# Cross-attention phase of a decoder layer: memory and token transposes moved from TensorE to DRAM round trips and VectorE

## The reference, cut to what matters

```
x   = x + attn(layernorm(x), ...)                          # phase A
x   = x + xattn(layernorm(x), ctx_1024, mask, ...)         # phase B
x   = x + ffn(layernorm(x), ...)                           # phases C and D

def xattn(x, mem_seq, mem_mask, rms_scale, q_w, kv_w, out_w):
    xn, mn = rmsnorm(x, rms_scale), rmsnorm(mem_seq, rms_scale)
    q      = rope(xn @ q_w) * HEAD_DIM**-0.5               # 4 heads of 128
    k, v   = mn @ kv_w ;  k = rope(k)                      # one head
    probs  = softmax(where(mem_mask, q @ k.T, MASK_FILL))
    return (probs @ v) @ out_w
```

## Time and profile before

| | |
|---|---|
| median of 3 runs | 3075.41 us (3075.34 to 3076.96) |
| the profiled execution | 3076.55 us, its span 3074.8 us |
| TensorE busy | 3035.9 us, 99% |
| VectorE busy | 1889.9 us, 61% |
| ScalarE busy | 1272.4 us, 41% |
| GpSimd busy | 830.7 us, 27% |
| phase A, 27 to 826 us | TensorE 797.1 of 799.0 us, VectorE 617.0, DMA engines 53% busy |
| phase B, 826 to 1860 us | TensorE 1014.5 of 1034.0 us, VectorE 801.9, ScalarE 665.2, GpSimd 634.2 |

### The profile page before, as it was taken

How to read it: one execution, slowest core, us unless ns; L and a number is a source line. 1 busy time by engine, 2 the same in 40 slices (tenths; PEclk the granted TensorE clock), 3 DMA queues, 4 the chain that set the end, 5 groups by cost and what they waited for, 6 DMA issues and landing times.

```text
span 3074.8 us, 40217 instructions
## 1 busy us (share of the span) xinstructions
PE 3035.9 (99%) x15124; PEld 2559.6 (83%) x15124; DVE 1889.9 (61%) x4077; ACT 1272.4 (41%) x2419; POOL 830.7 (27%) x699
## 2 busy tenths in 40 slices
PE   8999999999999999999999989999999999999999
PEld 7888888888878888888888878888888888888887
DVE  6777878777687778877877775343323343332455
ACT  4434343434366667666666652221211221112243
POOL 0101010101256666666666640000000000000144
PEclk9999999999999999999999999999999999999999
DMA  4545555555512121212111232111111112111486
GB/s 151 141 148 141 151 138 151 137 156 132 173 70 71 56 96 58 71 56 98 63 64 69 71 110 69 55 55 53 58 42 42 41 57 55 54 28 45 141 291 225
DMA packets 229729, 298.32 MB, mean 97 GB/s; under 512 B 12960, under 2 KB 109216, under 8 KB 229536
## 3 DMA queue, kind: packets, MB, share of 16 engines
q1 hardware_dynamic: 229536, 295.76, 31.7%
HBM read 183.52 MB, written 97.52 MB: 91 GB/s over the span
## 4 chain that ended last, share of the span: by engine, by line
PE 96%; DVE 2%; issue 1%; ACT 1%; DMA 0%; POOL 0%; SPq 0%; DVEq 0%; ACTq 0%
PE c_p L130 11%; PE c_p L132 11%; PE c_p L131 11%; PE a_p L130 6%; PE a_p L131 6%; PE a_p L132 6%; PE b_n L130 5%; PE b_n L132 5%; PE b_n L131 5%; PE b_t L1679 3%; PE d_p L132 2%; PE d_p L131 2%; PE d_p L130 2%; PE a_p L990 2%; PE a_r L132 2%; PE a_r L130 2%
## 5 line engine op out<-in xcount | busy, mean ns | idle before, releaser
L1299 POOL TENSOR_SCALAR b_soft<-b_soft,b_one_in_sum 128x512 f32<-128x512 f32 x256 | 401.8, 1571 | 298.9 <-DVE b_one_in_sum L1482 298.9
L1933 ACT ACTIVATE c_gate<-c_p,c_bias 128x512 f32<-128x512 f32 x180 | 124.2, 690 | 682.5 <-PE c_p L132 682.5
L1963 DVE TENSOR_TENSOR c_gate<-c_gate,c_gate 128x512 f32<-128x512 f32 x64 | 44.2, 690 | 502.7 <-ACT c_gate L1933 502.7
L1501 DVE TENSOR_TENSOR b_p_lo<-b_t,b_p_hi 128x512 fp32r<-128x512 f32 x256 | 175.1, 684 | 159.1 <-ACT b_p_hi L1356 156.5
L1347 ACT ACTIVATE b_soft<-b_soft,b_minus_top 128x512 f32<-128x512 f32 x256 | 185.2, 723 | 181.0 <-DVE b_minus_top L1493 176.4
L351 POOL TENSOR_TENSOR kept_scale<-c_ln_ve,minus_half 128x4 f32<-128x4 f32 x16 | 16.2, 1010 | 880.0 <-DVE c_ln_ve L343 880.0
L1356 ACT ACTIVATE b_p_hi<-b_t 128x512 fp32r<-128x512 f32 x256 | 151.8, 593 | 107.6 <-PE b_t L1679 107.6
L617 ACT ACTIVATE a_elu<-a_p 128x512 f32<-128x512 f32 x128 | 75.6, 590 | 282.0 <-PE a_p L132 282.0
L351 POOL TENSOR_TENSOR a_ln_sc<-a_ln_ve,minus_half 128x4 f32<-128x4 f32 x16 | 16.3, 1019 | 626.8 <-DVE a_ln_ve L343 626.8
L1493 DVE CUSTOM_DVE_ANT_0 b_soft<-b_l,b_mask_row 128x512 f32<-128x512 f32 x256 | 175.2, 684 | 0.0
L1679 PE MATMUL b_t<-ident,b_soft 128*128 128x128 f32 x1024 | 154.3, 273 | 12.2 <-DVE b_p_lo L1501 11.1
(11 more groups left out here) (297 smaller groups left out, 9520.6 us busy)
## 6 DMA issues: line engine op xcount, KB each, us to landing
a_res<-in_x SPq DMA_DIRECT2D x16, 1024.0 KB, 6.5
x<-a_res SPq DMA_DIRECT2D x16, 1024.0 KB, 5.2
b_mem<-in_ctx SPq DMA_DIRECT2D x16, 1024.0 KB, 5.4
b_x<-x SPq DMA_DIRECT2D x16, 1024.0 KB, 5.5
b_res<-x SPq DMA_DIRECT2D x16, 1024.0 KB, 5.5
x<-b_res SPq DMA_DIRECT2D x16, 1024.0 KB, 4.5
c_x<-x SPq DMA_DIRECT2D x16, 1024.0 KB, 5.6
d_x<-x SPq DMA_DIRECT2D x16, 1024.0 KB, 5.6
```

What stands on the lines that cost most here:

```text
L1299: pool.tensor_scalar(soft[:, at, :], soft[:, at, :], one_in_sum[:, at:at + 1], None, ALU.mult).then_inc(p_norm.sem, p_norm.unit)
L1501: dve.tensor_tensor(part.low, pT_bank[:, :].rearrange("p (i s) -> p i s", i=T), part.high_f32(), ALU.subtract).then_inc(p_lo.sem, p_lo.unit)
L1933: act.activation(gate[j % 2][i][:, :], gating.banks[(3 * j + i) % 6][:, :], ACT.Tanh if g == "c" else ACT.Sigmoid, bias=added[:, i, j:j + ...
```

## The change

In phase A, ScalarE squares the memory of each batch as it comes from DRAM (only the row sums are kept), while a second, shuffled copy is loaded; VectorE turns it with four 32x32-transpose instructions, and it is stored turned, not scaled, to DRAM (`x2`). The shuffled tokens of phase A go back into `x` itself and the shuffled attention output into `att`. One GpSimd pair of instructions makes the memory's scales of all batches.

In phase B the turned memory is loaded into `memT_f`, split into `memT` in slots 6 to 9 (high, ScalarE), 9 and 10 (low, chunks 0 and 1, GpSimd) and 14 and 15 (low, chunks 2 and 3, VectorE), and `keys_values(0)` waits for all four. Its scale is applied to the keys and values: `values_high` becomes four ScalarE instructions of 128 columns with a scale operand in place of one of 256. The rotation of the keys reads `k_scaled`, in SBUF, in place of the PSUM bank.

The tokens of batches 1 to 15 are normalised by ScalarE (slot 15, two tiles, and slot 0, two tiles), stored to DRAM, read back shuffled into `x`, turned by VectorE into `nT_f` in slots 5 to 8 ahead of `p_low`, and split: high by ScalarE in slots 5 to 8, low by GpSimd in slots 6, 7 and 8 (two in slot 8). Batch 0 is turned by TensorE as before. The larger jobs are placed anew.

```
-            Q, MEM = KT + 1, KT + 1 + H
+            Q = KT + 1
             jobs = [(k_rope, 2, 0), (k_rope, 6, 0)]
             for t in range(T):
                 jobs += [(xT_lo, t, 0), (x2_sb, t, 2)]
-            jobs += [(k_lo, 0, 0)] + [(q_cos, h, 0) for h in range(H)] + [(memT_lo, c, -1) for c in range(C)]
+            jobs += [(k_lo, 0, 0)] + [(q_cos, h, 0) for h in range(H)]
...
+            def shuffle_x(sp, b):
+                sp.wait_ge(N.normed.sem, N.normed.upto(b))
+                sp.dma_start(self.token_rows(self.out, b), x[:, :, :]).then_inc(x_moved.sem, x_moved.unit)
+                sp.wait_ge(x_moved.sem, x_moved.upto(b - 1, 0))
+                self.load_shuffled(sp, x, self.out, b, x_moved)
...
+                    def tokens_low(c):                      # GpSimd
+                        pool.wait_ge(xT_hi.sem, xT_hi.upto(new.b, c))
+                        pool.tensor_tensor(nT.low[:, c, :], nT_f[:, c, :], nT[:, c, :].high_f32(), ALU.subtract).then_inc(xT_lo.sem, xT_lo.unit)
...
                     for j in range(J):                      # GpSimd
                         if old and j < J - 1:
                             normalise(old.b, j + 1)
...
+                            if new.b >= 1 and 6 <= j <= 8:
+                                tokens_low(j - 6)
+                                if j == 8:
+                                    tokens_low(C - 1)
...
-                            if j == 9:
+                            if j == 10:
                                 query_sin(new.b, 0)
...
+                            if j == 9 or j == 10:
+                                memory_low(pool, after, j - 9)
...
+                            act.activation(v[new.par].high[:, t, :], bank[:, i, HD:2 * HD], ACT.Copy, scale=mem_scale[:, new.b, t:t + 1]).then_inc(v_hi.sem, v_hi.unit)
+                            act.activation(k_scaled[:, t, :], bank[:, i, 0:HD], ACT.Copy, scale=mem_scale[:, new.b, t:t + 1]).then_inc(v_hi.sem, v_hi.unit)
...
                         dve.wait_ge(v_hi.sem, v_hi.upto(new.b, 4 * g + 3))      # VectorE, keys(g)
...
                         if new and j == J - 1:              # VectorE
                             one_over(new.b, 0)
+                        if new and new.b >= 1 and 5 <= j <= 8:
+                            tokens_turned(j - 5)
                         if old and j >= 1:
                             p_low(old.b, j - 1)
...
+                            if j >= 14:
+                                memory_low(after, j - 12)
...
+                        if g == 0:                          # TensorE, keys_values(g)
+                            pe.wait_ge(mem_lo.sem, mem_lo.upto(new.b))
...
                         if new and j == 2:                  # TensorE
-                            keys_values(1)
+                            keys_values(1, (0,))
...
+                        if new and j == 3:
+                            keys_values(1, (1,))
+                        if fin and outs <= j < outs + T:    # outs is 4
+                            out(j - outs)
...
-                        if old and j == 7:
-                            encode(old, 0)
                         if new and j == 7:
                             turn_keys()
-                        if new and j == 8:
+                        if old and j == 8:
+                            encode(old, 0)
+                        if new and j == 9:
                             queries(0)
-                        if new and j == 9:
+                        if new and j == 10:
                             queries(1)
-                        if old and j == 10:
+                        if old and j == 11:
                             encode(old, 1)
-                        if new and j == 11:
+                        if new and j == 12:
                             queries(2)
...
+                        if after and j == 13:
+                            queries(3, (0, 1))
+                        if after and j == 14:
+                            queries(3, (2, 3))
...
-                        if following(new, B) and j in (13, 14):
-                            turn_memory(pe, s, new.b + 1, 2 * (j - 13))
-                            turn_memory(pe, s, new.b + 1, 2 * (j - 13) + 1)
```

More of the change, by code:

```diff
@@ L648, in step @@
                         weight_high(WQ, 2)
+                        for t in range(T):
+                            memory_square(act, new.b, t)
                     for c in range(C):
@@ L799, in step @@
                         weight_low(WP, 2)
+                        memory_turned(dve, new.b)
                     if old:
@@ L1307, in query_low @@
                         pool.tensor_tensor(q.low[:, h, :], rope[:, h % 2, :], q[:, h, :].high_f32(), ALU.subtract).then_inc(q_lo.sem, q_lo.unit)
+                    after = new.b + 1 if following(new, B) else None
+                    older_goes_on = old and following(old, B)
                     for j in range(J):
@@ L1438, in step @@
                                 query_high(new.b, 3)
-                        if new and 4 <= j <= 7:
-                            tokens_high(j - 4)
-                        if after and j >= 14:
-                            memory_high(act, s, after, 2 * (j - 14))
-                            memory_high(act, s, after, 2 * (j - 14) + 1)
+                            first = 4 if new.b == 0 else 5
+                            if first <= j < first + C:
+                                tokens_high(j - first)
                         if old and j < J - 2:
@@ L1554, in step @@
                     after = new.b + 1 if following(new, B) else None
+                    older_goes_on = old and following(old, B)
+                    sums = 5 if old else 4
                     for j in range(J):
@@ L1726, in turn_keys, with queries @@
                         mm.then_inc(kT_ps.sem, kT_ps.unit)
-                    def queries(h):
-                        bank = bank_of(Q + h)
-                        for c in range(C):
+                    def queries(h, chunks=range(C)):
+                        bank = bank_of(Q + h) if chunks[0] == 0 else turns.bank(s, Q + h)
+                        for c in chunks:
                             if h == 0:
@@ L1733, in queries @@
                             mm = product(pe, bank[:, :], qw[:, c, h * HD:(h + 1) * HD], nT[:, c, :], c == 0, c == C - 1)
-                        mm.then_inc(q_ps.sem, q_ps.unit)
+                        if chunks[-1] == C - 1:
+                            mm.then_inc(q_ps.sem, q_ps.unit)
+                    after = new.b + 1 if following(new, B) else None
+                    outs = 4 if old else 3
                     for j in range(J):
```

405 lines of the change are left out of this document (201 added, 204 removed).

## The result

The changed kernel takes 3124.32 us (median of 4 runs, 3122.74 to 3126.27) against 3075.72 beside it: ratio 1.0158, 95% interval 1.0146 to 1.017, slower by 48.6 us. The forecast was 3091, in a range of 3050 to 3110: the sign is right, the time lies outside the range. The profiled execution took 3125.27 us, its span 3123.5.

The account below looks back on a forecast made before the run. The prediction took TensorE's own queue, busy 99%, as the bound. From the profiled 3076.55 us, - 55.7 + 41 + 19 + 11 = 3091.9, so 3091 for the median, slower by 0.5%, in a range of 3050 to 3110.

Parts of the forecast that it names:

- What is removed: TensorE's memory and token transposes, 27.8 and 26.4 us, plus a 1.5 us wait for memory's split: gain at most 55.7 us.
- (a): Slot 7: `turn_keys` waits for GpSimd's low part of token chunk 2, 2.7 us in 15 steps, 41 us.
- (b): Slot 2: `turn_p(2)` waits for a late `p_low(1)`, 1.35 us in 14 steps, 19 us.
- (c): Slot 0: `keys_values(0)` waits for VectorE's low part of memory chunk 3, 0.7 us, 15 times, 11 us.
- What is hidden: Phase A's added squares, transposes and DMA, and phase B's token round trip, cost nothing; up to 1 us a phase A step.
- Rival 1: Slot 7's bank wait does not bite: 3050, or 3029 with the other waits at lower bounds; chance 0.15.
- Rival 2: Slot 7's wait bites, but those of slots 2 and 0 lie at their lower bounds: 3070; chance 0.19.
- Rival 3: Tokens' DRAM round trip comes late at `tokens_turned(0)`, slot 5; 15 us per us late, 3122 at 2 us; chance 0.08.

Follow-up runs that it names:

- experiment 11: Changed kernel with the repairs of experiment 1, experiment 4 and experiment 7 together, memory's low parts left in slots 14 and 15: 3041.16 us.
- experiment 1: Changed kernel, but bank bookkeeping skips the tokens' jobs 2, 4, 6, 8 from step 1 on, so `turn_keys` no longer waits for `xT_lo`: 3070.83 us.
- experiment 7: On top of experiment 1, memory's keys and values parted: keys scaled and rotated in slot 1, values' high and low parts in slot 2, slot 4 likewise: 3047.94 us.
- experiment 9: On top of experiment 1, experiment 4 and experiment 7, VectorE writes memory's low part 2 in slot 9 and part 3 in slot 14: 3032.56 us.
- experiment 5: On top of experiment 1, VectorE writes memory's low part of chunk 3 in slot 14 behind chunk 2, not in slot 15: 3067.97 us.
- experiment 4: Changed kernel, but the loads of memory 0 stand behind the load of batch 1's tokens in SyncE's queue: 3117.31 us.
- experiment 3: Changed kernel, but in GpSimd's slot 8 the low part of token chunk 2 stands ahead of `normalise(9)`: 3082.28 us.
- experiment 10: Changed kernel, but GpSimd does the memory's low part 0 in slot 8 ahead of token chunks 2 and 3, lengthening the `turn_keys` stall: 3151.42 us.
- experiment 6: On top of experiment 1, `values_high(0)` and `keys(0)` moved from slot 1 to slot 2: 3056.63 us.

## Why the prediction was wrong

By its own steps:

- **What is removed**, 0.87 and 0.44 us each time: right in the steady steps. Free of (a) and (b) a step is 57.87 (experiment 11) with (c) still in it, 0.64: 57.23 would be left, and 60.69 - 1.74 - 1.76 = 57.19. In step 1 the tokens' part bought nothing: it has no `out` products, and its slots 1 to 6, where the loop through `p_low` and `exp` sets the pace, took 18.24 before and 18.23 after. The prediction took every transpose at its spacing in a steady step.
- **(a)**, 2.7 us: right, 2.75 in steps 2 to 15, by the very chain that was written down. In step 1, whose slots are shorter and where TensorE was at the lower clock (granted 0.50 from 905 to 915 us), the slot took 8.71 (4.37 before, 3.27 in experiment 1).
- **(b)**, 1.35: right, 3.95 against 2.56, 1.39. Its cause was given as the end of `encode(fin, 3)` and more ScalarE work, and both are there: `p_low(1)` starts 3.22 after t(1), 0.95 later than before (2.27), by the added instructions, and ends at +3.89 (forecast 3.9). Of the two the waiting is the one that can be taken away: with the same work and no wait experiment 7 has `p_low(1)` at +1.27. Four ScalarE instructions started 0.25 apart, under the 0.3 that I took.
- **(c)**, 0.7: the size is right, 4.64 against 4.00, in part by luck. Changed kernel, between steps 5 and 6 (t(14) is 1194.33):

```profile
1197.43 0.94 DVE L1549 TENSOR_TENSOR b_memT_lo<-b_memT_f,b_memT_hi 128x512 fp32r<-128x512 f32 x1
...
1198.52 0.35 PE L130 MATMUL b_n<-b_kvw_hi,b_memT_hi 128*128 128x256 f32 x1 [0.39 <-DVE b_memT_lo L1549]
```

  The low part ends at +4.04: the chain's 3.8 and 0.25 more, 0.94 against 0.69 in slot 14. It begins 0.28 behind the start of GpSimd's `normalise`; beside no GpSimd instruction it took 0.68 (experiment 9). The prediction weighed in up to 0.9 for that, from a row beside a GpSimd instruction with two inputs in SBUF, which `normalise` is not, and took a value between. Beside one with two, in experiment 5, the same subtraction took 1.78 and ended 0.54 behind GpSimd's end; here it lost some 0.25 and did not wait for the end of `normalise`, which came 0.35 later than its own.
- **What is hidden**: the step that failed. "Phase A gets per step four ScalarE squares, four VectorE transposes and 3 MB of DMA [...] I take nothing" looked at a middle step, and there it holds: TensorE has no new wait. But SyncE's queue before the first step was not read, though 2 MB are put ahead of the tokens of batch 1 there. Forecast were 4.3 us less up to step 1, measured 8.5 more. Of these 12.8 us, 9.3 are there when TensorE waits for `a_att` (79.65 against 70.38), and experiment 4's order takes all of them away (69.66). What the order costs differs from run to run: 7.0 by the medians, 8.0 by the mean starts of step 1, and this trace, 4.1 later than the mean of its kind, is the dearest of eight. The other 3.5 arise behind that wait: just ahead of step 1 `keys_values` stands 2.5 us for the memory's low part, where (c) had 0.7, and the rest is not taken apart. "Phase A shows no new wait of TensorE" was wrong at the start, by the 5.67 us for `a_Wq_lo`.
- **Not in the sum at all**: the granted clock. The prediction priced a wait at its own length. Here a TensorE idle of 2.54 us brought half clock behind it in 5 of 13 steady steps, about 8 us, and over the doses the falls grew with the idle stretch: none of 13 behind 0.35 us (experiment 3), all 13 behind 3.76 (experiment 10). No single one of these explains the miss of 33 us: 3124.3 less the start's 12.8 is 3111.5, less the clock's 8 it is 3116.3, both still over 3110. The rest of the miss is step 1 (7.7: slot 7 takes 4.3 more than before, slot 8, again at the lower clock, 1.7, the others 1.6 and nothing is saved), 1.8 in steps 2 to 14 (a step at full clock grew by 1.45, not 1.32), step 15 (1.2, which no run takes apart), and 2.0 behind, in which a slot of the last step, 5.54 us, fell to the lower clock too (3.94 in experiment 6), behind an idle of 2.58 us; what brings it there in some traces and not in others stays open.

Rival 1 put the bank wait at 41 us. Experiment 1 shows it worth about 51, by the clock and step 1. Rival 2 is out by (b) and (c) as measured, 1.39 and 0.64, far over their lower bounds. Rival 3 did not come: VectorE never stood for a DMA at `tokens_turned`.

## What to carry to other kernels

When a buffer's writer goes away, its place in the bookkeeping must go too: a wait for nothing, asked one slot early, cost about 51 us, nearly all of the 54 that taking out 496 transposes was to give. Price a stall of TensorE by its length and by the clock behind it (here 2.54 us idle, and about 1.6 more in 5 of 13 steps), and look for what can be asked one slot later, or be parted so that only the piece that must wait stands behind the wait. Read the start of a program as a stage of its own: a load put ahead of another in one queue costs only once, but here that was 7 us.

## What the runs showed of the hardware

I had not expected TensorE's clock to fall behind stalls this short. In 13 steady steps it fell in none behind 0.35 us idle, in none behind the 1.23 of `turn_p(2)`, in 5 behind 2.54 (again 5 in experiment 4) and in all behind 3.76, and each time the slot behind took 1.0 to 1.6 us more. A stop at the full clock also lengthened its slot by 0.16 to 0.25 us more than the idle that the profile shows (2.75 for 2.54, 1.39 for 1.23, 0.64 for 0.39, 0.57 for 0.35). What a VectorE instruction loses beside GpSimd depended on both instructions, each of 128x512. With two inputs in SBUF beside a GpSimd one with two, it ended 0.54 to 0.55 us behind GpSimd's end (the 1.78 of experiment 5, and the 1.58 that the prediction shows); beside `normalise` it took 0.94 when begun 0.28 behind its start and 0.69 when begun 1.03 behind (changed kernel, slots 15 and 14 of step 5). With an input in PSUM (`b_rope<-b_n,b_cos_q`) it took 0.68 with 1.2 us of such a GpSimd instruction still to run (kernel before and changed kernel).

Issuing also had a price: four shuffled loads of 256 KB, issued by the same line of the kernel, held SyncE's queue for 9.59 us at the start (above; the DMA share from 11 to 21 us is 1.04) and for 1.93 in phase B (at 1143.87, where the share from 1143 to 1146 us is 0.36).
